# MLP weights in longer runs: four units a group in place of six, first-layer columns in alternate threes, MLP loop unrolled

## What is computed

```python
xn = _rms_norm(x, norm_weight, RMS_EPS)               # x: [16, 36, 192]
tok = _l2_normalize(xn)
sl = _l2_normalize(slots) * scale[:, None]            # [64, 192]
logits = jnp.einsum('sd,btd->bst', sl, tok)
dispatch_w = jax.nn.softmax(logits, axis=-1)
combine_w = jax.nn.softmax(logits, axis=-2)
y = jnp.einsum('btd,bst->bsd', xn, dispatch_w)
y = jnp.einsum('sio,bsi->bso', fc1_weight, y) + fc1_bias   # fc1: [64, 192, 768]
y = jax.nn.gelu(y, approximate=False)
y = jnp.einsum('sio,bsi->bso', fc2_weight, y) + fc2_bias   # fc2: [64, 768, 192]
out = jnp.einsum('bsd,bst->btd', y, combine_w)
```

## Time and profile before

| what | value |
|---|---|
| median of 3 runs | 247.25 us (245.79 to 251.49) |
| span of the profiled execution, first to last instruction | 244.4 us |
| TensorE busy | 221.5 us (91%) |
| weights moved in the MLP's loop and before | 48 loads of 1,536 KB |
| all DMA traffic | 79.74 MB in 40,904 packets |
| mean granted TensorE clock | 0.970 |

### The profile page before, as it was taken

How to read it: one execution, slowest core, us unless ns; L and a number is a source line. 1 busy time by engine, 2 the same in 40 slices (tenths; PEclk the granted TensorE clock), 3 DMA queues, 4 the chain that set the end, 5 groups by cost and what they waited for, 6 DMA issues and landing times.

```text
span 244.4 us, 5457 instructions
## 1 busy us (share of the span) xinstructions
PE 221.5 (91%) x2268; PEld 157.2 (64%) x2268; DVE 67.4 (28%) x166; ACT 64.0 (26%) x160; POOL 44.2 (18%) x80
## 2 busy tenths in 40 slices
PE   6799999999998889978979979997997999799794
PEld 6789756777767737635548547764664675576472
DVE  0557346678766532011011002002000200200202
ACT  2443242454656734021021021003002100300300
POOL 7501268663534020000000000001000000000000
PEclk9999999999999999997999997997699999999999
DMA  6999999999800059999999999999999999999952
GB/s 164 266 240 400 393 373 380 398 394 373 306 1 3 0 174 409 388 373 384 400 387 373 385 402 388 374 385 402 388 373 386 401 388 373 385 402 387 373 208 72
DMA packets 40904, 79.74 MB, mean 326 GB/s; under 512 B 1096, under 2 KB 28344, under 8 KB 40696
## 3 DMA queue, kind: packets, MB, share of 16 engines
q1 hardware_dynamic: 40888, 79.52, 90.8%
HBM read 79.07 MB, written 0.44 MB: 325 GB/s over the span
## 4 chain that ended last, share of the span: by engine, by line
PE 70%; DMA 9%; SPq 8%; ACT 5%; issue 3%; DVE 3%; POOL 1%; DVEq 0%; ACTq 0%
PE ps L1263 12%; PE ps L1223 11%; PE ps L875 10%; SPq L270 8%; DMA ring<-in_L_ffn_fc_weight_dram 6%; PE ps L1203 6%; PE ps L881 5%; PE ps L995 4%; PE ps L950 3%; DMA ring<-in_x_dram 3%; ACT region_p L593 2%; PE ps L968 2%; PE ps L1193 2%; PE ps L1239 2%; PE ps L907 2%
## 5 line engine op out<-in xcount | busy, mean ns | idle before, releaser
L875 PEld LDWEIGHTS ps<-ident 128*128 128x128 f32 x310 | 40.3, 208 | 10.6 <-issue 8.6
L875 PE MATMUL ps<-ident 128*128 128x128 f32 x310 | 44.9, 301 | 1.8 <-POOL neg_half L307 1.8
L846 DVE TENSOR_TENSOR region_p<-ps,b1T 128x384 f32<-128x384 f32 x16 | 8.2, 553 | 124.0 <-PE ps L1239 124.0
L1263 PE MATMUL ps<-ring,region_p 128*32 128x192 f32 x768 | 37.8, 352 | 1.2 <-ACT region_p L608 0.9
L1263 PEld LDWEIGHTS ps<-ring,region_p 128*32 128x32 f32 x768 | 24.9, 119 | 11.7 <-ACT region_p L608 2.7
L1223 PE MATMUL ps<-ring,qkvT 128*32 128x384 f32 x288 | 26.8, 490 | 0.0
L593 ACT COPY region_p<-ps 128x384 f32<-128x384 f32 x16 | 11.7, 831 | 55.3 <-PE ps L1223 55.3
L1203 PE MATMUL ps<-region_k,soft_space 128*108 128x192 f32 (+1 forms) x96 | 18.6, 336 | 0.4 <-ACT region_k L610 0.4
L1203 PEld LDWEIGHTS ps<-region_k,soft_space 128*108 128x108 f32 (+1 forms) x96 | 13.7, 163 | 7.1 <-issue 6.3
L429 POOL COPY qkvT<-region_k 128x384 f32 x6 | 3.1, 513 | 79.8 <-PE ps L1223 79.8
L1239 PE MATMUL ps<-ident,region_p 128*128 128x128 f32 x48 | 7.0, 282 | 11.4 <-ACT region_p L593 11.4
(11 more groups left out here) (137 smaller groups left out, 235.1 us busy)
## 6 DMA issues: line engine op xcount, KB each, us to landing
ring<-in_L_ffn_fc_weight_dram SPq DMA_DIRECT2D x48, 1536.0 KB, 15.9
ring<-in_x_dram SPq DMA_DIRECT2D x2, 864.0 KB, 8.8
ring<-in_L_tok_W_proj_dram SPq DMA_DIRECT2D x1, 576.0 KB, 7.7
ring<-in_L_attn_w_qkv_dram SPq DMA_DIRECT2D x1, 432.0 KB, 11.2
out_dram<-h SPq DMA_DIRECT2D x2, 162.0 KB
ring<-in_L_ffn_fc_bias_dram SPq DMA_DIRECT2D x1, 192.0 KB, 9.5
ring<-in_L_attn_w_proj_dram SPq DMA_DIRECT2D x1, 144.0 KB, 11.7
soft_space<-in_L_tok_pos_emb_dram SPq DMA_DIRECT2D x3, 27.0 KB
```

The costliest lines, as they stand in the source:

```text
L846: dve.tensor_tensor(pre[:, 3 * half:3 * half + 3, :].rearrange("p c (s b) -> p c s b", s=GS), ps[:, 2 + half, 0:384].rearrange("p (c s b) ...
L875: pe.matmul(ps[:, bank, 0:128], ident[:, :], ident[:, :], start=True, stop=True)
L1263: mm = pe.matmul(ps[32 * q:32 * q + 32, 4, 0:D], gact[:, 2 * u + cc, 2 * q + l, :], w[:, 2 * q + l, cc, :], start=first, stop=last, tile_p ...
```

## The change

A group's weights come as four units of 2.25 MB. The two first-layer units each hold two slot pairs with all three rows 3p to 3p+2 (one run of 2,304 floats, 9,216 bytes, in a partition and pair). The two second-layer units each hold every second slot with all six rows 6p to 6p+5 (a run of 1,152 floats, 4,608 bytes). The ring has 8 slots of the new size, the same bytes as before. A unit of the first layer now yields a whole bank: the four strips are two pairs times two halves of the 768 hidden columns, and a half takes three of every six neighbouring columns (`w[:, qq, j, :, 3 * hf:3 * hf + 3]`). So each bank is copied, transposed and activated by itself (`first_layer`, `turn_hidden`, `keep_hidden`, `activate`). The Gelu is four instructions of 192 columns in place of two of 384. The bias table `b1T` is laid out to match and takes two copies. Groups are all written out, `y_group` and its copies are gone, and the numbers of `keep_busy` are others: 8, 12 and 12 a group from group 1 on, without the last 12 in group 7.

```diff
-    UNITS = 6
+    UNITS = 4
     RING = 2 * UNITS
-    UF = GS * D * FF // 3 // 128
+    UF = GS * D * FF // 2 // 128
...
-        fc1_view = fc1_w.rearrange("s d o -> (s d) o").rearrange("(q p j) o -> j p q o", p=128, j=3)
-        fc2_view = fc2_w.rearrange("s (p c) d -> p s c d", p=128)
+        fc1_view = fc1_w.rearrange("s d o -> (s d) o").rearrange("(q p j) o -> p q (j o)", p=128, j=3)
+        fc2_view = fc2_w.rearrange("(q l) (p c) d -> l p q (c d)", l=2, p=128)
...
+            def keep_hidden(g, pr):
+                act.wait_ge(units_used, g * UNITS + pr + 1)
+                earlier(act, hid_turned, 2 * (g - 1) + pr + 1 if g else 0)
+                act.copy(hid[:, pr, :, :].rearrange("p c n -> p n c"),
+                         ps[:, pr, 0:FF // 2].rearrange("p (n c) -> p n c", c=3)).then_inc(hid_ready, 1)
...
+            for g in range(GROUPS):
+                if g == 0:
...
+                keep_hidden(g, 0)
+                if g:
+                    activate(g, 0)
+                keep_hidden(g, 1)
...
+                activate(g, 1)
+                act.wait_ge(units_used, (g + 1) * UNITS)
+                act.copy(y2[:, g % 2, :], ps[:, 4, 0:D]).then_inc(y2_ready, 1)
...
+            def first_layer(g, pr):
+
+                if g and pr == 0:
+                    pe.wait_ge(mix_ready, g)
+                slot = g * UNITS % RING + pr
+                pe.wait_ge(unit_in[slot], 16 * (g * UNITS // RING) + 16)
+                w = ring[:, slot, :].rearrange("p (q j n c) -> p q j n c", q=2, j=3, c=FC)
                 for j in range(3):
...
+                    for qq in range(2):
+                        for hf in range(2):
+                            k = 2 * qq + hf
+                            mm = pe.matmul(ps[32 * k:32 * k + 32, pr, 0:FF // 2],
+                                           y_diag[:, j, 4 * g + 2 * pr + qq, :],
+                                           w[:, qq, j, :, 3 * hf:3 * hf + 3],
+                                           start=(j == 0), stop=(j == 2), tile_position=(0, 32 * k))
+                mm.then_inc(units_used, 1)
...
+            for g in range(GROUPS):
+                first_layer(g, 0)
+                if g == 0:
+                    turn_logits()
+                else:
+                    combine(g - 1, 1 - g % 2)
+                    turn_hidden(g, 0)
+                first_layer(g, 1)
+                if g == 0:
                     turn_combine()
...
+                    turn_hidden(g, 0)
+                turn_hidden(g, 1)
...
+                mix_weights(g, g % 2)
+                if g:
+                    keep_busy(4, 8)
+                second_layer(g, 0)
+                if g:
+                    keep_busy(3, 12)
+                second_layer(g, 1)
+                if 0 < g < GROUPS - 1:
+                    keep_busy(3, 12)
             combine(GROUPS - 1, 1)
```

More of the change, by code:

```diff
@@ L109, in vit_tower_kernel @@
         slotT = sb("slotT", [128, 2, S])
[L110 removed]
+        b1T = sb("b1T", [128, 3, S // 2, 4])
         b2_rows = sb("b2_rows", [128, D])
@@ L419, in _ @@
             pool.memset(gact[:, :, :, :], 0.0).then_inc(gact_zero, 1)
[L422 to L432, removed]
+            for g in range(2, GROUPS):
+                pool.wait_ge(mix_done, g - 1)
+                select(g, g % 2)
         @block.scalar
@@ L1207, in combine @@
                         mm.then_inc(combined, 1)
[L1209 to L1215, removed]
-                for j in range(3):
[L1217 to L1233, removed]
-                    turn_combine()
[L1236 to L1241, removed]
@@ L1245, in mlp_group @@
                         open_output(t)
[L1246 to L1255, removed]
-                    w = ring[:, slot, :].rearrange("p (s c d) -> p s c d", s=GS, c=2)
-                    pe.wait_ge(unit_in[slot], it * 16 + 16)
-                    for cc in range(2):
-                        for l in range(2):
-                            for q in range(4):
-                                first = u == 0 and cc == 0 and l == 0
-                                last = u == 2 and cc == 1 and l == 1
-                                mm = pe.matmul(ps[32 * q:32 * q + 32, 4, 0:D], gact[:, 2 * u + cc, 2 * q + l, :],
-                                               w[:, 2 * q + l, cc, :], start=first, stop=last,
-                                               tile_position=(0, 32 * q))
-                    mm.then_inc(units_used, 1)
-            for gg in range(2):
-                mlp_group(gg, gg, 0)
-            with pe.Fori(1, GROUPS // 2) as it:
-                for gg in range(2):
-                    mlp_group(it * 2 + gg, gg, it)
+                mix_weights(g, g % 2)
[7 more added lines that the diff above has]
+                    keep_busy(3, 12)
             combine(GROUPS - 1, 1)
```

110 lines of the change are left out of this document (63 added, 47 removed).

## The result

The changed kernel took 262.11 us (median of 4 runs, 261.65 to 264.64). Its ratio to the kernel before, run beside it on the same chip, is **1.066, 95% interval [1.062, 1.070]**: slower by 6 to 7%. The ratio goes by fast executions alone, and two of the four of the kernel before (250.79 and 251.49 us) were slow. On the median of 247.25 us from which the prediction started it is 263.5 us, at the very end of the range; the middle value was 257.8. The profiled executions have spans of 259.9 and 244.4 us, 15.5 apart, where the sum said 10.5. So direction and mechanism held, and 5 us are missing in the sizes.

The account below looks back on a forecast made before the run. Weight transfers and TensorE's program bound the kernel together; afterwards TensorE alone. Group 0 +0.4, group 1 +5.4, groups 2 to 6 +10.4, low clock -4.65, group 7 -1.05: +10.5 on 247.25 makes 257.8 us, range 252.0 to 263.5.

Parts of the forecast that it names:

- the sum: TensorE's program: a group's parts added to 21.64 us, and the changes over all groups to +10.5 us.
- What bounds the kernel before: In the MLP, weight transfers (until 237.04 us) and TensorE's program (until 236.96) end together; TensorE waited 0.12 us.
- The transfers after: MLP weight loads in longer runs: 422 and 411 GB/s, last unit landing at 227.1 us, or 237.8 without gain.
- The straight line: Weight-load packet time drawn through two run lengths: 9.2 ns + 0.0369 ns a byte, giving 422 and 411 GB/s.
- TensorE's group, 21.64: One MLP group at full clock, from start to start: 21.64 us, 2.08 more than before.
- Strided columns: First layer reading three floats and skipping three: taken as 0 extra, upper end 12%, +4 us.
- The dummies: MLP `keep_busy` calls, 212 where there were 126, stand in TensorE's program at 0.2475 us each.
- Rival 1: In the MLP, transfers are the bound and `keep_busy` is free: 9.9 us earlier, 237.4 us; chance 0.06.
- The pipelined hidden layer: First layer of each group: TensorE's idle for ScalarE's copies falls from 1.57 to 0.96 us, giving 0.61.
- The low clock: MLP stretches at lower clock, 4.65 us in excess, taken as all gone since they follow idle time for ScalarE.
- rival 2: The MLP's lower clock stays: +15.2 to 16.5 us, 262.5 to 263.7; chance 0.20 together with strides costing.
- Rival 3: First-layer strides cost up to 4 us: 262; chance 0.20 together with the lower clock staying.

## Why the prediction was right or wrong

**What bounds the kernel before: right.** Without its dummies it takes the same time (ratio 1.000), so the transfers alone hold it; with 0.93 us a group more on TensorE it became slower (1.016 [1.009, 1.022], a small change, in part hidden by a better clock), so TensorE holds it too. Reading TensorE's timeline against the chain gave this; the chain names one of two. The wait that the prediction put at 0.12 us is 0.20 by the starts: nine calls and the step to the second layer take 237.08 - 234.68 = 2.40 us there, and 2.20 in group 6.

**The transfers after: right in size.** The straight line gave 422 and 411 GB/s and a last load at 227.1. The slices show 407 to 427, and the end at 226 with an MLP that began 0.6 us earlier. The 358 GB/s that the prediction quoted from the Trainium skill ("DMA: Bandwidth & Descriptors", Bandwidth) is passed here by every kernel (387 and 416 over more than 100 us). The same section gives about 358 for each of two cores that share HBM, the chip's memory, when both stream, and a measured 425 for one that streams alone. One core runs this program, and the trace agrees with the second figure: 407 to 427 by the slice. The slower TensorE did not hold them up through the ring: they ended some 25 us ahead of its last unit.

**TensorE's group, 21.64: 0.74 too low, and that is the failure.** The step that failed is "Strided columns ... I take 0, as the row is almost at the same price", with its upper end of 12%. Measured: 567 ns for 486, 17% an instruction and 0.95 us a group. The row behind it reads every second float, and for that the runs show 500 ns, 3%: it was a fair row for another pattern. Threes cost 81 ns where single floats cost 14. The prediction's own sign of being wrong came with it: a first-layer call, two instructions, takes 0.21 us and not under 0.18. By groups, against the predicted end of the second layer at 248.9 (measured 251.75 + 2.09 = 253.8): groups 1 to 6 are 6 x 0.74 = +4.4, group 7 is 19.51 for 18.70, +0.8, group 0 is 15.2 for 14.9, +0.3, and the MLP began at 84.89 for 85.49, -0.6: +4.9 in all, the missing 5 us. Within a group the threes' +0.95 was partly covered by 0.21 that the sum had too high elsewhere, as the group of 21.43 with one piece shows. Most of that is `keep_busy`, 8.06 us in the sum and 1.98 + 2.88 + 2.88 = 7.74 measured; the other parts came out 0.1 longer together. With the threes priced at 0.95 the sum would have been 2.7 us too high and not 4.9 too low.

**The dummies: right in mechanism**, 10% too dear a call. Rival 1 (dummies free, 237.4) fails as named: TensorE never waited for a load in the kernel after.

**The pipelined hidden layer: right.** Idle 0.94 for 0.96, once a group, and no wait for the Gelu.

**The low clock: right in size, its cause not shown.** The prediction took all 4.65 us as gone and they went; rival 2 did not come. That the cure was the shorter idle time and not the added dummies is supported by the kernel with 126 calls (0.986 to 1.000, before 0.956 to 0.986 with as many), but its dummies also stand in other places. Against it stands the kernel before with threes, which lost the same 4.65 us with the old idle time and the old dummies. So the reason that the prediction gave is argued and not shown, and that the whole 4.65 went may be luck.

**Rival 3 (strides, up to 4 us)** named the right place and had too low a ceiling: with the threes' 0.95 in eight groups it is 7.6. No part of the fetch or the unrolling showed a price: the groups are equal to 0.02 us.

## What to carry to other kernels

When a chain ends on a load, look whether the engine that took it had waited: here it was 0.2 us, and a faster load could gain nothing until TensorE's program was made shorter. Dummy matmuls that keep the clock up gained nothing here beside loads that bound the kernel (without its 126 the kernel before took the same time), and what didn't fit beside the loads cost its full time (19.4 us for 86 calls). Where the low clock did cost, behind the last load (2.6 us in one execution), no run tried them. A moving operand in another pattern should be measured in that very pattern before it is put on a path with no slack.

## What the runs showed that was not expected

- A 384-column f32 matmul in four strips took 486 ns from one piece, 486 from alternate fours, 485 from sixes, 500 from pairs or single floats, and 567 from threes.
- Without dummies the granted clock fell to 0.908 to 0.930 in the mean (kernel before, ten runs) and cost nothing, as TensorE still had to wait for its last load.
- Profiles of kernels whose code is the same ahead of the MLP differ by up to 3 us there (the versions of the changed kernel began it at 84.6 to 87.8 us), which is more than some of the edits were worth; the spans have to be compared from the start of the MLP.
